# The dispatch of a mixture of experts in two parts: three samples' full blocks first, the last sample's between the blocks

## The chip, the cores and the metric

The kernel runs on one core of a Trainium2 chip. The metric is the device time of one execution in microseconds (us). PE (TensorE) multiplies and transposes, DVE (VectorE) and ACT (ScalarE) evacuate PSUM and do the elementwise work, POOL (GpSimd) does some elementwise work and issues the indirect gathers and scatters, and SP (SyncE) issues the plain DMAs. Each engine runs its own instructions in order, and semaphores join them.

## The reference, cut to what matters

The input x is 4 samples of 1024 positions with 256 channels. Three layers follow one another:

```python
x = x + softmax(theta(x) @ phi(x).T) @ g(x) @ W_out + b_out      # in each sample, width 32
t = t + nystrom_attention(layernorm(t))                         # 8 heads, 128 landmarks, 6 steps of an inverse
# mixture of experts: T = 4096 tokens, E = 16 experts, K = 2
xf = layernorm(t)
probs = softmax(xf @ W_gate); top_g, top_i = top_k(probs, 2)
for e in range(16):
    y += gates[:, e] * (gelu(xf @ W1[e]) @ W2[e])               # 256 -> 512 -> 256
t = t + y
```

Each sample's attention needs that sample alone. The inputs are seeded, so it can be counted which experts the 8192 picks go to. Picks of experts 0 to 15 in all four samples: 269 371 331 470 957 915 584 865 786 425 263 770 232 441 313 200. Of these in the first three samples: 221 285 242 373 703 665 451 696 577 333 203 515 171 332 230 147. A block is 128 picks of one expert, so there are 73 blocks that hold picks (3 3 3 4 8 8 5 7 7 4 3 7 2 4 3 2 by expert), and the kernel always runs 79.

## The kernel before, in words

For each sample `i` three stages of 8 tiles follow one another. Stage one (`s` from 0 to 9, lines L1234 to L1375) is the first attention: PE multiplies scores (L637), DVE takes the maxima (L1234), ACT the exponentials (L1074), PE turns them (`transposes`, L545), ACT copies them (L1087), PE multiplies with the values (L719) and DVE finishes the row and its norm (`rows0`, `norm0`). Stage two is the Nystrom attention's landmarks: the same pattern per head, and between its steps in each slot `s` up to four pieces of the iterative inverse (`inverse_piece`, L871 on PE, L1489 and L1490 on DVE). In each slot DVE also does a step of the routing of the sample before (`top_two`, `index`, `picks`, `one_hots`, `either`, `counted`). A slot of PE waits at `values` for `pr_used`, that is for DVE's L1499 of the head before. Stage three applies the landmarks to the 8 tiles: eight small exponentials per tile on ACT (L1079), `inverses` on DVE, `turn_inverses` on PE (L698), which spreads 8 reciprocals over 256 rows by sixteen small matmul instructions, `out_t`, `rows1` (L1386), statistics, a deviation on POOL (L400, L401), and `norm1` (L1357).

After the last sample comes the dispatch. The last rows are turned, gated (L608, L617) and routed. The picks of all 32 tiles are ranked (L961 to L967), DVE works out where each expert's blocks begin and where each pick goes (L1597 to L1617), and for 8 steps of four tiles DVE, ACT and PE build one-hot rows and multiply them into a table that says which pick stands in which row of which block (`select`, L1629 to L1634, and `place`, L977). Out of that come `token_of`, `row_of` and `expert_of`. PE runs transposes that nothing uses while it waits (lines before L985).

Then 79 blocks run, sorted by expert. For block `n` POOL gathers 128 rows (L434), PE turns them, DVE copies them (L1678), PE multiplies with W1 (L1008, `hidden`), ACT applies Gelu (L1174) and stages the next W1 (L1165), PE multiplies with W2 (L1017, `rows_out`), DVE scales by the gate (L1695), and POOL adds the rows to the output in memory by a scatter (L448). The gather of block n+4 stands ahead of the scatter of block n in POOL's queue. Blocks of one expert never hold the same token, so their scatters may be under way together. The first of another expert must wait until all scatters of the experts before it have landed; the first 8 blocks wait for the one before each. From block 8 on SP watches the landings (L537) and lets POOL go on by `scatter_ok`. All experts' weights (16 of 1 MB) are loaded by SP, more than half of them after the last sample, into memory that the attention has used.

## Time and profile before

| | us |
|---|---|
| median of 3 runs (range) | 990.86 (990.32 to 993.77) |
| the profiled execution | 986.97 |
| its span, first to last instruction | 985.2 |
| PE busy | 902.3 (92%) |
| DVE busy | 559.1 (57%) |
| ACT busy | 448.1 (45%) |
| POOL busy | 298.1 (30%) |

The busy time of an engine is summed over the span. The stages have different limits, so the time is read stage by stage: windows give the busy time in a stretch, and the timeline gives each instruction with the idle time of its engine before it and what ended that.

### The profile page before, as it was taken

What the parts mean: (1) busy time and instruction counts of PE and PEld (TensorE: products, weight loads), DVE (VectorE), ACT (ScalarE), POOL (GpSimd) and SP (SyncE); (2) the same over time, 40 slices, a digit from 0 to 9 for tenths busy, and PEclk for the clock granted to TensorE, in tenths of its full rate; (3) what the DMA queues carried; (4) which work ended last, traced back from release to release, by engine and by line L of the source; (5) the groups of instructions that cost most, each with busy time, mean ns of one, the idle gap of its engine ahead of it and who ended that gap; (6) DMA issues with size and microseconds to landing.
All of it is one profiled execution on the core that took longest, in us unless ns stands there. A gap on an engine that the chain in (4) does not pass through costs nothing.

```text
span 985.2 us, 21923 instructions
## 1 busy us (share of the span) xinstructions
PE 902.3 (92%) x7118; PEld 700.4 (71%) x7119; DVE 559.1 (57%) x1581; ACT 448.1 (45%) x1004; POOL 298.1 (30%) x343
## 2 busy tenths in 40 slices
PE   5999989899999899999899999638999999999997
PEld 3566767565767565777656676428889999999996
DVE  3577857677857588766678775694222222222222
ACT  2524367534358443348452347334434444444442
POOL 3150001060001041001131000103576676666665
PEclk9699999999999899999899999857999999999999
DMA  3100000300000200000206004581344434434341
GB/s 107 44 2 1 1 1 24 107 1 1 1 2 16 85 31 2 1 2 2 72 15 214 1 1 151 152 256 36 52 65 71 69 63 72 67 62 67 61 64 19
DMA packets 47848, 50.78 MB, mean 52 GB/s; under 512 B 11072, under 2 KB 41152, under 8 KB 47776
## 3 DMA queue, kind: packets, MB, share of 16 engines
q0 software_dynamic: 15168, 18.85, 12.1%
q1 hardware_dynamic: 32608, 30.99, 10.0%
q8 instruction: 43, 0.70, 0.3%
q14 instruction: 29, 0.24, 0.1%
HBM read 33.00 MB, written 18.78 MB: 53 GB/s over the span
## 4 chain that ended last, share of the span: by engine, by line
PE 79%; DVE 13%; issue 4%; ACT 3%; DMA 1%; POOL 1%; POOLq 0%; DVEq 0%; ACTq 0%
PE PS L1008 14%; PE PS L1017 14%; PE PS L545 12%; PE PS L871 7%; PE PS L574 6%; PE PS L637 4%; PE PS L738 3%; PE PS L648 3%; PE PS L642 3%; DVE neg_max L1234 3%; PE PS L719 3%; PE PS L724 2%; ACT arena L1079 1%; PE PS L733 1%; DVE arena L1222 1%
## 5 line engine op out<-in xcount | busy, mean ns | idle before, releaser
L400 POOL TENSOR_SCALAR aggr<-aggr 128x1 f32<-128x1 f32 x64 | 14.2, 222 | 517.8 <-DVE aggr L1354 517.8
L1234 DVE TENSOR_REDUCE neg_max<-PS 128x1 f32<-128x1024 f32 (+1 forms) x96 | 117.5, 1224 | 79.5 <-PE PS L648 27.4
L545 PE MATMUL PS<-ident,arena 128*128 128x128 f32 x1008 | 142.0, 289 | 19.4 <-DMA arena<-in_x_dram 6.5
L1008 PEld LDWEIGHTS PS<-low 128*128 128x128 f32 x1264 | 153.3, 192 | 4.6 <-DVE low L1678 0.6
L545 PEld LDWEIGHTS PS<-ident,arena 128*128 128x128 f32 x1008 | 123.7, 151 | 45.9 <-issue 36.9
L1008 PE MATMUL PS<-low 128*128 128x128 f32 x1264 | 153.8, 275 | 0.4 <-DVE low L1678 0.4
L1017 PE MATMUL PS<-arena,low 128*128 x632 | 150.0, 380 | 3.0 <-ACT low L1174 1.8
L448 POOL DMA_INDIRECT out_dram<-low,row_of x79 | 125.4, 1587 | 81.1 <-DVE low L1695 30.3
L1087 ACT COPY arena<-PS 128x1024 f32<-128x1024 f32 x96 | 98.4, 1025 | 86.9 <-PE PS L545 86.9
L1017 PEld LDWEIGHTS PS<-arena,low 128*128 128x128 f32 x632 | 114.0, 190 | 16.7 <-issue 4.4
L1174 ACT ACTIVATE low<-PS 128x512 f32<-128x512 f32 x79 | 47.2, 597 | 157.8 <-PE PS L1008 157.7
L1074 ACT ACTIVATE arena<-PS,neg_max 128x1024 f32<-128x1024 f32 x64 | 71.3, 1114 | 96.2 <-DVE neg_max L1234 96.2
L434 POOL DMA_INDIRECT low<-rows_scratch,token_of x79 | 78.1, 988 | 64.2 <-DVE token_of L1651 38.8
L1079 ACT ACTIVATE arena<-PS,neg_max 128x128 f32<-128x128 f32 x256 | 90.4, 399 | 7.6 <-DVE neg_max L1234 7.6
L1695 DVE TENSOR_SCALAR low<-PS,slot_gate 128x256 f32<-128x256 f32 x79 | 38.2, 483 | 97.3 <-issue 64.9
L1165 ACT COPY low<-arena 128x1024 f32 x79 | 82.4, 1045 | 18.2 <-issue 14.4
L1676 DVE TENSOR_TENSOR gate_parts<-low,pick_of 128x2 f32<-128x2 f32 x79 | 12.7, 161 | 125.1 <-PE PS L545 125.1
L871 PE MATMUL PS<-arena 128*128 128x256 f32 x320 | 74.4, 386 | 0.0
L871 PEld LDWEIGHTS PS<-arena 128*128 128x128 f32 x320 | 59.1, 190 | 11.2 <-issue 4.0
L574 PE MATMUL PS<-arena,low 128*128 128x512 f32 x128 | 61.7, 606 | 4.5 <-DVE arena L1492 2.6
L1051 ACT ACTIVATE arena<-PS 128x512 f32<-128x512 f32 x40 | 23.7, 595 | 83.4 <-PE PS L574 40.2
L1079 ACT ACTIVATION_READ_ACCUMULATOR arena<-PS,neg_max 128x1 f32 x256 | 60.9, 238 | 0.0
(216 smaller groups left out, 1310.3 us busy)
## 6 DMA issues: line engine op xcount, KB each, us to landing
arena<-in_L_ffn_W_dram SPq DMA_DIRECT2D x32, 512.0 KB, 8.4
arena<-in_x_dram SPq DMA_DIRECT2D x4, 1024.0 KB, 6.3
out_dram<-t SPq DMA_DIRECT2D x4, 1024.0 KB, 7.3
rows_scratch<-arena SPq DMA_DIRECT2D x4, 512.0 KB, 4.1
rows_scratch<-arena SPq DMA_DIRECT2D x8, 256.0 KB, 2.7
low<-rows_scratch,token_of POOLq DMA_INDIRECT x79, 2.8
out_dram<-low,row_of POOLq DMA_INDIRECT x79, 3.8
arena<-in_L_attn_w_qkv_dram SPq DMA_DIRECT2D x1, 768.0 KB, 4.8
```

Source lines behind the costliest of these rows:

```text
L434: pool.indirect_dma_start(xg[:, n % 4, :], None, rows_dram, bass.IndirectOffsetOnAxis(ap=token_of[:, n:n + 1], axis=0)).then_inc(xg_loaded ...
L448: pool.indirect_dma_start(out_rows, bass.IndirectOffsetOnAxis(ap=row_of[:, n:n + 1], axis=0), y_sb[:, n % 4, :], None, bounds_check=T - 1, ...
L545: mm = pe.transpose(PS[0:s.shape[1], dst_bank, n * P:n * P + s.shape[0]], s, ident[0:s.shape[0], 0:s.shape[0]])
L574: mm = pe.matmul(PS[0:m, bank, :], w[c], src[:, c, half * 512:half * 512 + 512], start=c == 0, stop=c == KC - 1)
L871: mm = pe.matmul(bank[:, o:o + 2 * M], RX[:, g, h, 0, :], RX[:, g, h].rearrange("p r m -> p (r m)"), start=True, stop=True)
L1008: mm = pe.matmul(PS[:, 2 + p, hc * P:(hc + 1) * P], w1_now[:, p, c * H + hc * P:c * H + (hc + 1) * P], xgT[:, p, c, :], start=c == 0, stop ...
L1017: mm = pe.matmul(PS[:, 6 + p, 0:D], hT[:, p, c, :], w2_sb[:, bass.ds(e * (HC * D) + c * D, D)], start=c == 0, stop=c == HC - 1)
L1074: act.activation(Pm[:, u % 2, :], src, ACT.Exp, bias=neg_max[:, u % 2, 0:1], accum_out=row_sum[:, u % NT:u % NT + 1]).then_inc(s_exp, 1)
L1079: ins = act.activation(Pm[:, u % 2, o:o + M], src[:, o:o + M], ACT.Exp, bias=neg_max[:, u % 2, h:h + 1], accum_out=head_sum[:, u % 2, h:h ...
L1087: act.copy(PT[:, u % 2, :], PS[:, 2:4, :].rearrange("p b n -> p (b n)")).then_inc(t_act, 1)
L1165: act.copy(w1_now[:, p, :], w1_sb[:, bass.ds(e * (KC * H), KC * H)]).then_inc(w1_staged, 1)
L1234: dve.tensor_reduce(dst, src, AX.X, ALU.max, negate=True).then_inc(s_max, 1)
```

## The change

The 24 tiles of the first three samples are dispatched during the last sample. Each expert's picks among them fill `floor(count/128)` full blocks, 40 by the counts above (1 2 1 2 5 5 3 5 4 2 1 4 1 2 1 1); at least 32 (`SURE`) whatever the inputs. The picks that fill no block stand aside and join the picks of the last sample in the late blocks (33 of them hold picks: 2 1 2 2 3 3 2 2 3 2 2 3 1 2 2 1). The blocks run in this order, early ones of experts 0 to 15 and then late ones of experts 0 to 15. Ranks of the early picks are taken between stages one and two of the last sample, their one-hot rows are made by DVE and multiplied out by POOL (`early_vals`) in stage two, and PE places them there (six times eight matmuls). The tables for 32 blocks are made in stage three, and POOL gathers the first four blocks there. The routing of each sample is done in stage one of the next. The first 20 blocks are written out, and between them PE, ACT and DVE do what is left of the last sample: turning, gate, routing, ranks, one-hot rows and the second table. The weights are loaded in an order that follows the experts, nine of them before the blocks begin; most buffers move in memory for that. In stage three POOL spreads the reciprocals over 256 columns and PE turns them as two squares of 128; `rows1` and `norm1` stand earlier in a tile and its statistics are split in two. The transposes that nothing uses are gone.

```diff
+    OPEN = 5
...
+        EARLY = TT - NT
+        FULL = 2 * EARLY * P // P
+        SURE = (2 * EARLY * P - E * (P - 1)) // P
+        SURE = SURE - SURE % 4
+        EARLY_COLS, LATE_COLS = FULL + E, COLS - SURE
...
+            def early_vals(k):
+
+                b, mine = k % 2, slice(k * 2 * ST, (k + 1) * 2 * ST)
+                pool.wait_ge(hot_made, k + 1)
+                if k >= 2:
+                    pool.wait_ge(sel_used, k - 1)
+                pool.tensor_tensor(hot_val[b], hot_hi[b].unsqueeze(1).broadcast_to([P, 2, 2 * ST, EARLY_COLS]),
+                                   vals[:, :, mine].unsqueeze(3).broadcast_to([P, 2, 2 * ST, EARLY_COLS]), ALU.mult).then_inc(vals_made, 1)
...
+                def spread_inverses(t):
+
+                    pool.wait_ge(inv_ready, i * NT + t + 1)
+                    if t >= 2:
+                        pool.wait_ge(inv_mm, i * NT + t - 1)
+                    by_place = head_inv[:, t % 2, :].rearrange("p (a g b) -> p g a b", g=NG, b=2)
+                    for g in range(NG):
+                        pool.tensor_copy(inv_spread[:, t % 2, g * P:(g + 1) * P].rearrange("p (a b d) -> p a b d", a=2, b=2),
+                                         by_place[:, g].unsqueeze(3).broadcast_to([P, 2, 2, HD])).then_inc(inv_spread_ready, 1)
+
...
+                    if i == B - 1 and t == NT - 4:
+
+                        pool.wait_ge(tokens_ready, 1)
+                        pool.wait_ge(gates_stored, 16)
+                        pool.wait_ge(xn2_stored, 16 * 3 * (B - 1))
+                        pool.wait_ge(q_mm, B * 4)
+                    if i == B - 1 and NT - 4 <= t < NT:
+                        gather(t - (NT - 4))
...
+                    if n + 4 == SURE:
+
+                        pool.wait_ge(tokens_ready, 2)
+                        pool.wait_ge(gates_stored, 16 * 2)
+                        pool.wait_ge(xn2_stored, 16 * 3 * B)
+                        pool.wait_ge(out_stored, 16 * B)
...
+            i = B - 1
+
+            sp.wait_ge(s_mm, i * UNITS + 3)
+            sp.wait_ge(tpg_mm, 2 * B)
+            sp.wait_ge(xb_ready, B)
+            store_out(i - 1)
+            both_in(0, 1)
+
+            sp.wait_ge(s_mm, i * UNITS + NT)
+            sp.wait_ge(pr_used, i * UNITS + NT)
+            sp.wait_ge(g_ready, B)
+            both_in(2, 3)
+
+            sp.wait_ge(gates_made, 1)
+            sp.dma_start(gate_cols[:, 0:EARLY], gates[:, 0:EARLY]).then_inc(gates_stored, 16)
+
+            sp.wait_ge(pv_mm, i * UNITS + 2 * NT)
+            both_in(4, 5)
+
+            sp.wait_ge(y_head_mm, B)
+            sp.wait_ge(sel_used, EARLY // ST)
+            both_in(6, 7, 8)
+            store_rows(i, 0, 4)
+            loaded(range(9))
+
+            sp.wait_ge(s_mm, B * UNITS)
+            both_in(9)
+            first_in(10)
...
+            sp.wait_ge(gates_made, 2)
+            sp.dma_start(gate_cols[:, EARLY:TT], gates[:, EARLY:TT]).then_inc(gates_stored, 16)
 
             sp.wait_ge(release_ready, 1)
-            with sp.Fori(IN_TURN, BLOCKS) as n:
-                landed = [sp.value_load(release[0:1, bass.ds(n, 1), u:u + 1].rearrange("p o u -> p (o u)"), min_val=16,
-                                        max_val=16 * (ROUNDS + 1)) for u in range(4)]
-                for u in range(4):
...
-                    for g in range(NG):
-                        for j in range(QUADS):
-                            h = g * GH + j
-                            mm = pe.matmul(PS[HD * j:HD * j + HD, 0, g * P:(g + 1) * P], head_inv[:, t % 2, PLACE[h]:PLACE[h] + 1].broadcast_to([P, HD]),
-                                           ident[:], start=True, stop=True, tile_position=(0, HD * j))
-                    mm.then_inc(inv_mm, 1)
...
+                def early_place(k):
+
+                    pe.wait_ge(vals_made, k + 1)
+                    pe.wait_ge(pr_used, i * UNITS + NT + k + 2)
+                    if k == 0:
+                        pe.wait_ge(starts_made, 1)
+                        pe.transpose(PS[0:1, 0, 288:288 + BW], block_expert[0:BW, :], ident[0:BW, 0:BW])
+                    for j in range(2 * ST):
+                        mm = pe.matmul(PS[:, 0, 512 - 2 * EARLY_COLS:512], hot_lo[k % 2][:, j, :], hot_val[k % 2][:, :, j, :],
+                                       start=j == 0, stop=j == 2 * ST - 1)
+                    mm.then_inc(sel_used, 1)
...
+            aside = {0: lambda: turn_high(B - 1), 2: lambda: gate(B - 1), 4: lambda: gate_turned(B - 1), 9: late_ranks,
+                     12: late_turns, 17: late_place}
...
+            pe.wait_ge(pr_used, B * UNITS)
             turn_rows(1, 0, 1)
             hidden(0, 0, False)
-            for u in range(4):
-                expert_block(0, u, False)
-            with pe.Fori(1, ROUNDS) as i:
+            for r in range(OPEN):
+                for u in range(4):
+                    expert_block(r, u, r >= 1)
+                    if 4 * r + u in aside:
+                        aside[4 * r + u]()
+            pe.wait_ge(tables_ready, 2)
...
+            def late_exps():
+
+                act.wait_ge(probs_in, 2)
+                act.activation(probs_b, probs_b, ACT.Exp)
+                act.activation(gates[:, EARLY:TT], gates[:, EARLY:TT], ACT.Exp).then_inc(probs_exp, 1)
+
+            aside = {0: lambda: bulk(23, xT[:, 1, 512:1024], j=B - 1), 8: late_exps}
...
+                def early_starts():
+
+                    dve.wait_ge(rank_mm, 1)
+                    for j in range(B - 1):
+                        dve.tensor_copy(run_a[:, j * NT:(j + 1) * NT], PS[:, 1, j * E * NT:(j + 1) * E * NT].rearrange("p (e t) -> p t e", t=NT))
+                    alone(dve.tensor_copy(col_e[:, 0, :], PS[:, 1, EARLY * E:EARLY * E + E]))
+                    dve.memset(small[:, 43:44], 0.0).then_inc(rank_read, 1)
+                    alone(dve.tensor_copy(col_ei[:], col_e[:, 0, :]))
...
+                def early_added(k):
+
+                    dve.wait_ge(sel_used, k + 1)
+                    src = PS[:, 0, 512 - 2 * EARLY_COLS:512].rearrange("p (a n) -> p a n", a=2)
+                    if k == 0:
+                        dve.tensor_copy(expert_row[0:1, 0, :], PS[0:1, 0, 288:288 + BW])
+                        dve.tensor_copy(early_parts[:], src).then_inc(sel_added, 1)
+                    else:
+                        dve.wait_ge(sel_added, k)
+                        dve.tensor_tensor(early_parts[:], src, early_parts[:], ALU.add).then_inc(sel_added, 1)
+
+                def early_hot(k):
+
+                    b, mine = k % 2, slice(k * 2 * ST, (k + 1) * 2 * ST)
+                    over_row = lambda ap, n: ap.unsqueeze(1).broadcast_to([P, 2 * ST, n])
+                    over_col = lambda ap, n: ap.unsqueeze(2).broadcast_to([P, 2 * ST, n])
+                    if k >= 2:
+                        dve.wait_ge(vals_made, k - 1)
+                        dve.wait_ge(sel_used, k - 1)
+                    dve.tensor_tensor(hot_lo[b], over_row(iota_lo[:], P), over_col(pos_lo[:, mine], P), ALU.is_equal)
+                    dve.tensor_tensor(hot_hi[b], over_row(iota_hi[:, 0:EARLY_COLS], EARLY_COLS), over_col(pos_hi[:, mine], EARLY_COLS),
+                                      ALU.is_equal).then_inc(hot_made, 1)
+
+                def route(s):
+
+                    if s == 3:
...
+                def route(s):
+
+                    if s == 3:
+                        for t in range(NT):
+                            top_two(i, t)
+                    elif s in (4, 5):
+                        for t in range(4 * (s - 4), 4 * (s - 4) + 4):
+                            index(i, t)
+                    elif s == 6:
+                        picks(i)
+                        keep(i)
+                    elif s == 7:
+                        one_hots(i)
+                    elif s == NT:
+                        either(i)
+                    elif s == NT + 1:
+                        counted(i)
+
...
+                def early_steps(s):
+
+                    if s == 0:
+                        early_run()
+                    elif s == 1:
+                        alone(positions(run_a, weighed_a, early, slice(0, 2 * EARLY)))
+                    elif s == 2:
+                        early_hot(0)
+                    if 2 <= s < EARLY // ST + 1:
+                        early_hot(s - 1)
+                    if s == 3:
+                        dve.wait_ge(kept, B - 1)
+                        gates_in(probs_a, early, slice(0, EARLY))
+                    elif s == 7:
+                        dve.wait_ge(probs_exp, 1)
+                        gates_out(probs_a, slice(0, EARLY))
+
...
+            aside = {0: lambda: bulk(22, xT[:, 0, 512:1024], j=B - 1), 1: lambda: releases(0, IN_TURN, release_early[:, IN_TURN:SURE]),
+                     3: lambda: gate_out(B - 1), 5: late_top, 6: late_index, 7: late_picks, 8: late_counts, 9: late_gates,
+                     10: late_starts, 11: late_run, 13: late_rest, 14: lambda: late_hots(0), 15: lambda: late_hots(1),
+                     18: late_tables, 19: lambda: releases(1, SURE, release_late[:])}
```

## Rows read from the trace of the kernel before

**Rows 1.** Windows: us; busy PE, PEld, DVE, ACT, POOL; clock, DMA, GB/s

```profile
603.43:619.50 16.07, 16.07 (x209) 12.49 (x210) 11.78 (x29) 15.49 (x71) 2.37 (x6) 1.00 0.33 107
...
553.39:578.70 25.31, 25.31 (x188) 19.16 (x184) 20.82 (x69) 8.87 (x12) 0.00 (x0) 1.00 0.00 1
...
351.00:357.00 6.00, 6.00 (x75) 3.93 (x73) 5.59 (x13) 3.95 (x7) 2.96 (x6) 1.00 0.01 3
...
740.00:960.00 220.00, 220.00 (x1533) 207.74 (x1533) 61.65 (x236) 96.87 (x118) 151.88 (x118) 1.00 0.42 66
...
320.00:340.00 20.00, 16.71 (x91) 10.35 (x88) 12.00 (x23) 7.75 (x13) 2.37 (x6) 0.83 0.12 42
```

**Rows 2.** Timeline of PE: start, us, engine, line, operation, tiles, count, idle before

```profile
340.65 1.05 PE L608 MATMUL PS<-arena,wgate_sb 128*32 128x256 f32 x16
...
605.95 0.62 PE L698 MATMUL PS<-ident,head_inv 128*32 128x128 f32 x16
...
607.47 1.04 PE L545 MATMUL PS<-ident,arena 128*128 128x128 f32 x8
...
629.41 1.03 PE L738 MATMUL PS<-low 128*128 128x256 f32 x4
...
654.35 1.22 PE L977 MATMUL PS<-low 128*128 128x160 bf16 x8 [8.42 <-ACT low L1142]
...
678.27 3.84 PE L1008 MATMUL PS<-low 128*128 128x128 f32 x32 [0.37 <-DVE low L1678]
```

**Rows 3.** Timeline, DVE, end of the last sample

```profile
630.48 0.42 DVE L1386 TENSOR_TENSOR t<-PS,arena 128x256 f32<-128x256 f32 x1
...
632.91 0.41 DVE L1357 TENSOR_SCALAR arena<-t,aggr 128x256 f32<-128x256 f32 x1 [0.80 <-POOL aggr L401]
```

**Rows 4.** Timeline, PE and then DVE, in stage two of the last sample

```profile
559.14 0.64 PE L719 MATMUL PS<-arena 128*32 128x128 f32 x16
...
558.58 0.25 DVE L1499 TENSOR_SCALAR low<-PS,row_inv 128x32 f32<-128x32 f32 x1
```

**Rows 5.** Timeline, DVE, operations of the dispatch

```profile
638.98 0.62 DVE L1280 MAX8 top_now<-logits_now 128x8 f32<-128x16 f32 x7
...
651.77 0.82 DVE L1629 TENSOR_TENSOR low<-iota_hi,pos_hi 128x640 bf16<-128x640 bf16 x1
...
652.52 1.22 DVE L1631 TENSOR_TENSOR low<-iota_lo,pos_lo 128x1024 bf16<-128x1024 bf16 x1
```

**Rows 6.** Timeline, POOL and then DVE, when both work in stage one

```profile
367.37 0.72 POOL L423 TENSOR_TENSOR arena<-arena,low 128x256 f32<-128x256 f32 x1
...
369.01 4.53 POOL L406 TENSOR_TENSOR arena<-arena,low 128x2048 f32<-128x2048 f32 x1
...
367.44 0.81 DVE L1357 TENSOR_SCALAR arena<-arena,aggr 128x256 f32<-128x256 f32 x1 [0.80 <-POOL aggr L401]
```

**Rows 7.** Timeline, POOL, scatters of the block stage

```profile
685.53 1.65 POOL L448 DMA_INDIRECT out_dram<-low,row_of  x1 [5.93 <-DVE low L1695]
...
703.73 1.59 POOL L448 DMA_INDIRECT out_dram<-low,row_of  x1 [1.78 <-DVE low L1695]
...
709.19 1.59 POOL L448 DMA_INDIRECT out_dram<-low,row_of  x1 [2.58 <-DMA out_dram<-low,row_of]
...
718.55 1.59 POOL L448 DMA_INDIRECT out_dram<-low,row_of  x1 [1.85 <-DVE low L1695]
...
765.74 1.59 POOL L448 DMA_INDIRECT out_dram<-low,row_of  x1 [0.96 <-DVE low L1695]
...
770.34 1.59 POOL L448 DMA_INDIRECT out_dram<-low,row_of  x1 [1.72 <-DVE gate_parts L1676]
...
773.52 1.59 POOL L448 DMA_INDIRECT out_dram<-low,row_of  x1 [0.30 <-issue]
```

**Rows 8.** Timeline, ACT, the change of its table

```profile
668.75 1.28 ACT L1156 ACT_TABLE_LOAD   x1
```

**Rows 9.** Timeline, SP, the store of the gates

```profile
650.70 1.38 SPq L529 DMA_DIRECT2D rows_scratch<-gates  x1
```

702 lines of the change are left out of this document (418 added, 284 removed).

## The prediction

> **What bounds the kernel now.** I read the windows first, stage by stage. In the block stage PE is busy for the whole of 740 to 960 us [rows 1]: 1533 matmul instructions at 26 per block (16 hidden, 2 turned, 8 out) are 59.0 blocks in 220.0 us, 3.73 us each, and 79 blocks at that rate are 294.7 us. Four slots of stage two of the last sample take 25.31 us, 6.33 each, with PE full and DVE busy for 20.82; in stage one DVE has 5.59 of 6.00 beside a full PE; four tiles of stage three take 16.07, 4.02 each, with PE full and ACT busy for 15.49 [rows 1]. So each stage is bound by PE, with DVE or ACT right behind it. The one place where nothing is near full is the dispatch. The PE timeline shows it: the last output projection starts at 629.41 and the first hidden layer at 678.27 [rows 2]. Those 48.9 us are what the change is after.
>
> **What goes.** After it the first hidden layer needs only the end of the attention. From the DVE timeline: row 7 of the last sample is added at 630.48, its norm starts at 632.91 (it waits for POOL) and ends near 633.3 [rows 3]. DVE then has a small product and one copy of 256 columns (0.42, as any such operation in [rows 3]) to do, and the split statistics move all by 0.1 to 0.3. That puts the hidden layer at 634.1 to 634.2, if tables, rows and weights are there, where it was 678.27: **-44.1**. The transposes that nothing uses lie inside this gap. The first weights are issued in stages one to three, and the first four gathers some 15 us early, so I cost them at nothing; the cover is that time.
>
> **What the block stage takes over.**
> - PE's moved work: sixteen gate matmuls at 1.05 [rows 2], eight transposes about 1.0 [rows 2], the smaller turns and ranks 1.0, and seventeen placements of 96 columns. Eight of 160 columns took 1.22 [rows 2] at half clock, so 1.4. Together 4.4, of which I count 3, since PE also stalls for scatters among the first ten blocks.
> - DVE's moved work: it has about 2.4 us free per block before the next block's copy is late (61.65 busy in 220 [rows 1] is 1.05 of 3.73, and the copy must be done when the hidden layer begins). `late_starts`, some twenty small chained operations, is about 4.3, so 1.9 late; `late_tables` 0.6 late. Total 2.5, from 0 to 6.
> - ACT needs exponentials again between two Gelus: two table loads at 1.28 [rows 8] plus 0.6, against some 1.8 free in a block: 1.5.
> - SP lets scatter 8 go only after it has sent the late gates, which DVE makes behind block 9. The store took SP 1.38 for 4096 rows [rows 9]. POOL's scatters and the gathers behind them wait: 2, from 0 to 7.
> - The clock: between 320 and 340 us a pause of 1.8 us was followed by a mean of 0.83 [rows 1], which is 6.8 us at half rate, 3.4 lost. The pause before the first block is over 3 us, so 3.5, from 0 to 4.
> - About 7 MB of weights and stores are still on their way when the first gathers and scatters start: 1, from 0 to 6.
> - **More changes of expert.** Order decides how often a scatter must wait for all landings before it. Before, the 79 blocks have 15 such changes, after it 31 (15 in the 40 early blocks, one between, 15 in the late). Scatter 21 is the first of expert 5: it starts 4.60 after scatter 20; the next, not a first, 3.18 later [rows 7], and 3.18 is POOL's own minimum. Against 3.73 a first loses 0.87 and another wins back 0.55. Blocks 28 to 72 have 23 firsts and 22 others: 23 x 0.87 - 22 x 0.55 = 7.9. How much backlog is free? In the first eight, each waiting for the one before, scatter 4 starts 18.20 after scatter 0 [rows 7], where four blocks are 14.9: 3.3 behind, and there PE first stalls, for a gather that stood behind the scatters. So 7.9 - 3.3 = 4.6.
>
> Sum: 3 + 2.5 + 1.5 + 2 + 3.5 + 1 + 4.6 = **+18.1**.
>
> The Trainium skill ("ScalarE: Activation LUTs", rules for kernel authors) budgets 2.7 us for every switch of set. The load here took 1.28 [rows 8]; with the page's figure this term would be 4.3 instead of 1.5.
>
> **What the last sample takes over.** In stage two PE and DVE hand over closely: W of a head is ready at 558.83 (L1499) and PE uses it at 559.14 [rows 4], so DVE has 0.3 us to spare, beyond the 0.6 of routing that now goes. `early_hot` is a comparison of 1024 and one of 512: 1.13 and 0.6 by the rows of 1024 and 640 less overlap [rows 5], 1.7 per step and two steps in slot 2. The excess over 0.9 falls on PE: 2.6 in slot 2, 1.7 in slot 3 (the gates are there too), 0.85 in each of slots 4 to 6, 0.2 in slot 7, together 7.1. The six placements on PE are 0.6 each, 3.5. `positions` in slot 1 (768 elements twice and six small ones, 2.75) costs 1.8, `early_run` in slot 0 0.9. Ranks and `early_starts` before stage two: DVE has gaps there, 0.8. The added sums at the end of stage two 0.9, `early_tables` with its dozen small operations on DVE in stage three 1. Sum **+16**, between 7 (DVE catches up in its waits) and 26 (POOL's multiplications are late: 2048 elements took 4.53 [rows 6], so 1024 about 2.4, and twice that would exceed its slot).
>
> **Routing in stage one** of samples 1 to 3. It brings eight maxima (seven took 0.62 [rows 5]), the indices and four products, near 4 us of DVE per sample, to the stage where DVE has 0.41 of 6.00 free [rows 1]. The stage ends in a wait for POOL of 0.8 [rows 6] and in smaller waits for PE, which hide the last steps, and PE runs up to 1.6 us ahead of DVE. I take 1.3 per sample, **+4**, from 0 to 9. In stage two, from which it goes, PE is the bound: nothing is won outside the last sample.
>
> **Stage three.** Sixteen instructions (0.62 busy [rows 2]) become two transposes: 1.04 for eight [rows 2], so 0.26. PE wins 0.2 to 0.3 a tile while PE is the bound, which is some four to five tiles of eight, and ACT stops it at about 3.8 of 4.02 us (15.49 in four tiles is 3.87 with overlaps, and no gap but a wait for DVE per tile [rows 1]): -1.0 per sample. POOL's two copies (0.45 each from 0.72 for 256 [rows 6]) come after the reciprocal and 2 us ahead of their use, also behind a deviation or a gather. The earlier `rows1` shortens the chain of the last three tiles by 0.5 per sample. **-6** in all, from -10 to +4.
>
> **Sum.** -44.1 + 18.1 + 16 + 4 - 6 = -12.0. The span of 985.2 becomes 973.2, the profiled execution 986.97 becomes 975.0. The median lies 3.9 above that execution; the same saving from it gives 990.86 - 12.0 = 978.9, say 979.
>
> **Rivals.**
> - *Most of the moved work is hidden* (chance 0.25). DVE's excess in stage two is taken up by its waits (7 for 16), the routing by the slack of stage one (0), the block stage takes 11: -44.1 + 11 + 7 + 0 - 6 = -32, 959 us. For it: DVE is busy for 20.82 of 25.31 in stage two [rows 1]. Against: the margin of 0.3 there.
> - *The scatters become the bound* (0.12, the slower side). If a first starts 5.5 us after the one before (as scatter 5, at 709.19, did after scatter 4, at 703.73; the first eight average 33.02 / 7 = 4.72 [rows 7]), 23 x 1.77 - 22 x 0.55 - 3.3 = 25.3 instead of 4.6, and the early blocks add some 4: 979 + 25 = 1004. It cancels the gain at 0.87 + 12 / 23 = 1.4 over 3.73, that is 5.1 between scatters; from 5.3 on the kernel is slower by 0.5%. Against: 4.60 once the backlog is gone.
> - *POOL holds stage two* (0.13). POOL's products and DVE's comparisons run at once. A norm that took 0.41 [rows 3] took 0.81 while POOL was multiplying [rows 6]. If the two lengthen each other so, the early hot rows take 4.8 on POOL and 3 on DVE, and six slots gain 1.6 each: +10, 989. The Trainium skill ("GPSIMD Engine Reference", key points) says that POOL shares its SBUF interfaces with VectorE, with contention when a DVE instruction has two SBUF inputs or runs in a 2-port mode; both comparisons have two such inputs. One row agrees so far.
> - *The change doesn't do what it says* (0.05): the first tables, weights or gathers are not there at 634 plus what the last sample has grown, and PE waits a further 10 to 20 us behind SP's queue: 989 to 999.
> - My forecast has 0.45.
>
> **How the numbers follow.** Forecast 979, its own range 970 to 988 from the bounds of its terms. For 8 in 10 I reach down to 962, short of the first rival's end, and up to 995. A measurement of this kernel can tell about 0.5%, 5 us, from no change. Faster than 985.9: nearly all of the first rival and 0.40 of my 0.45, and some of the third: 0.72. Within: 0.16. Slower than 995.8: the scatters and part of the last rival, 0.12.
>
> **What would show it.** In the profile of the changed kernel: the first L1008 of the blocks some 4 us after the last projection, with the clock at 0.5 for up to 7 us; slots of stage two in the last sample at 7.5 to 8 us instead of 6.33, with PE waiting for W; scatters near 4.6 apart in blocks 28 to 72 and PE waiting for gathers there; stage-three tiles at 3.8 instead of 4.0. The forecast is wrong if stage two keeps 6.9 us slots, if scatter spacing leaves 4.1 to 4.8, or if PE waits before the first block.

## The result, and the profile of the changed kernel

| | before | changed |
|---|---|---|
| median of 20 runs each, us | 990.25 | 994.50 |
| range | 985.65 to 997.06 | 990.83 to 997.88 |
| span of the profiled execution | 985.2 | 993.4 |

The ratio of the two is 1.0037, with a 95% interval of 1.0022 to 1.0053: a little slower, clear of no change, though by less than the 0.5% that I had named as the least a measurement can tell. I had forecast 979, 1.2% faster. Each ratio below is to the kernel before, run beside it on the same chip. The changed kernel itself did not run beside the variants, so "less than the changed kernel" is always the difference between a variant's ratio and 1.0037.

Some words that come back below: a maximum is DVE's first operation on a tile's or a head's scores, and a stage is measured from its first maximum to that of the next stage; a slot is the stretch from one maximum to the next, counted from 0; a first is a scatter that must wait until all before it have landed; the landing is the end of a scatter's transfer.

The gap in front of the blocks is gone as predicted. The timeline of PE in the changed kernel (columns: start, duration, engine, line, operation, tiles, count, idle time before and what ended it) answers [rows 2]. Its first six rows belong to the steps of stage two of the last sample:

```profile
start us, us, engine line op out<-in xcount [idle before <-releaser]
548.27 2.08 PE L1028 MATMUL PS<-arena 128*128 128x128 f32 x8 [2.15 <-DVE small L1773]
...
559.57 0.65 PE L852 MATMUL PS<-arena 128*32 128x128 f32 x16 [2.40 <-DVE low L1823]
...
570.29 0.29 PE L894 MATMUL PS<-ident,block_expert 80*1 80x80 f32 x1 [4.32 <-issue]
570.37 1.06 PE L896 MATMUL PS<-arena 128*128 128x128 bf16 x8
...
580.98 0.61 PE L896 MATMUL PS<-arena 128*128 128x128 bf16 x8 [1.51 <-DVE low L1823]
...
611.87 0.61 PE L896 MATMUL PS<-arena 128*128 128x128 bf16 x8 [2.19 <-DVE low L1823]
...
646.84 0.44 PE L680 MATMUL PS<-ident,inv_spread 128*128 128x128 f32 x2 [1.19 <-POOL inv_spread L491]
...
653.65 1.10 PE L871 MATMUL PS<-low 128*128 128x256 f32 x4
...
658.84 3.53 PE L1140 MATMUL PS<-low 128*128 128x128 f32 x21 [2.76 <-DVE low L1995]
```

The last projection starts at 653.65 and the first hidden layer at 658.84, 5.2 us later instead of 48.9. But 658.84 is only 19.4 us before the old 678.27, not 44: the samples have become longer. And from scatter 0 to scatter 78 the blocks take 320.5 us instead of 294.5.

**Where the samples grew.** Read by the starts of DVE's maxima. Stage two of the last sample took 51.5 us and takes 72.8. Stage one of samples 1 to 3 took 48.65, 49.86 and 50.02, and takes 52.06, 52.26 and 50.91 (+6.7 in these two traces; other traces of the same code sum to 150.7 instead of 148.5, and to 156.8 instead of 155.2). Stage three of samples 0 to 2 took 51.87, 52.22 and 51.87, and takes 49.22, 49.23 and 49.23 (-8.3); that of the last sample, from first to last maximum, 33.06 and now 36.42 (+3.4). Everything also starts 2.2 us later (first maximum at 19.73, before 17.56). The windows of slots 1, 2, 3 and 5 of stage two and of the whole stage answer the second window of [rows 1] (6.33 a slot, PE full):

```profile
core 0: us, PE busy (x) PEld busy (x) DVE busy (x) ACT busy (x) POOL busy (x), PEclk, DMA share, GB/s
546.39:559.34 12.95, 8.90 (x34) 5.84 (x34) 6.88 (x23) 2.81 (x4) 0.00 (x0) 0.74 0.00 0
559.34:570.10 10.76, 6.40 (x46) 4.82 (x46) 9.84 (x17) 2.22 (x3) 3.01 (x2) 0.91 0.01 2
570.10:580.75 10.65, 9.18 (x55) 6.86 (x55) 7.41 (x19) 2.22 (x3) 2.48 (x2) 0.77 0.00 0
590.25:598.12 7.87, 6.93 (x54) 5.26 (x54) 6.71 (x17) 2.22 (x3) 1.90 (x2) 1.00 0.01 3
533.18:605.98 72.80, 58.81 (x403) 42.12 (x403) 56.68 (x125) 20.99 (x31) 10.95 (x6) 0.88 0.00 1
```

The granted clock (the figure behind POOL's) was 1.00 there before. Now it is 0.74, 0.91 and 0.77 in three slots, and 0.82 in slot 4. Narrower windows show where it fell to the lower of its two levels, 1.2 instead of 2.4 GHz: inside PE's idle of 2.15 us, inside that of 4.32, and 0.8 us after the end of that of 1.51. It didn't fall after the idle of 2.40: PE's work in slot 2 ran at 2.4 GHz, and the 0.91 there comes from the idle of 4.32 at the slot's end. The eight placements show the two levels: 1.06 us at 570.37, and 0.61 at 580.98 and in the later slots. PE's work behind the idles of 2.15, 2.40 and 1.51:

```profile
548.27:554.00 5.73, 5.73 (x15) 3.66 (x16) 1.13 (x4) 0.79 (x3) 0.00 (x0) 0.50 0.00 0
559.57:565.97 6.40, 6.39 (x46) 4.79 (x46) 5.51 (x12) 2.22 (x3) 0.00 (x0) 1.00 0.01 3
580.98:585.00 4.02, 4.02 (x30) 3.03 (x31) 2.05 (x5) 1.75 (x4) 1.25 (x1) 0.60 0.00 0
```

**Where the blocks grew.** POOL's timeline, the scatters alone (L528), answers [rows 7]:

```profile
667.74 1.65 POOL L528 DMA_INDIRECT out_dram<-low,row_of  x1 [7.40 <-DVE low L2009]
...
675.05 1.59 POOL L528 DMA_INDIRECT out_dram<-low,row_of  x1 [4.36 <-DMA out_dram<-low,row_of]
...
682.90 1.58 POOL L528 DMA_INDIRECT out_dram<-low,row_of  x1 [4.97 <-DMA out_dram<-low,row_of]
...
707.84 1.59 POOL L528 DMA_INDIRECT out_dram<-low,row_of  x1 [1.79 <-DMA out_dram<-low,row_of]
...
716.44 1.59 POOL L528 DMA_INDIRECT out_dram<-low,row_of  x1 [5.71 <-SPq L664]
```

These are scatters 0, 1, 2, 7 and 8. The first intervals are 7.31 and 7.85, where four took 18.20 before. Two windows of the changed kernel, from the first hidden layer to scatter 0 and from scatter 0 to scatter 2 (the last three figures are clock, DMA share and GB/s):

```profile
658.84:667.74 8.90, 8.90 (x57) 8.64 (x58) 2.73 (x10) 3.39 (x5) 1.09 (x2) 0.81 1.07 364
667.74:682.90 15.16, 13.83 (x107) 12.09 (x105) 4.76 (x22) 7.51 (x11) 5.23 (x4) 1.00 0.94 283
```

The first stretch took 7.26 before, at a clock of 1.00: here the half clock costs some 1.6 ahead of scatter 0. In the second the weights are still loading.

Scatter 8 starts 8.60 after scatter 7 and is released by SP's L664 (the count of landings), which SP reached only after it had stored the late gates at 712.03. In the whole, scatters 0 to 8 take 48.7 us (before 36.2) and blocks 28 to 72 take 179.1 (before 168.4). The chain of work that ended last, by engine, in the kernel before and then in the changed one:

```profile
PE 79%; DVE 13%; issue 4%; ACT 3%; DMA 1%; POOL 1%; POOLq 0%; DVEq 0%; ACTq 0%
PE 65%; DVE 16%; issue 7%; DMA 6%; ACT 2%; POOL 2%; SPq 0%; POOLq 0%; DVEq 0%; ACTq 0%
```

What PE lost there went to transfers, to stretches in which nothing that the profile shows was waited for ("issue"), and to DVE.

### The profile page after: what moved, and what is told of

It is laid out like the page before. It is cut to its first block, busy times and chain, and to the rows that moved or that the text cites. A ratio compares the mean times of both kernels' runs of the same rounds, so it can differ in the third digit from the quotient of the medians.

```text
span 993.4 us, 20907 instructions
## 1 busy us (share of the span) xinstructions
PE 904.6 (91%) x6644; PEld 694.3 (70%) x6645; DVE 561.7 (57%) x1610; ACT 437.4 (44%) x975; POOL 332.4 (33%) x413
## 4 chain that ended last, share of the span: by engine, by line
PE 65%; DVE 16%; issue 7%; DMA 6%; ACT 2%; POOL 2%; SPq 0%; POOLq 0%; DVEq 0%; ACTq 0%
PE PS L1149 11%; PE PS L1140 11%; PE PS L680 11%; PE PS L1033 8%; PE PS L712 6%; DMA out_dram<-low,row_of 4%; DVE neg_max L1402 3%; PE PS L786 3%; PE PS L775 3%; PE PS L780 2%; PE PS L871 2%; PE PS L852 2%; DMA low<-rows_scratch,token_of 2%; PE PS L857 1%; ACT arena L1246 1%
## 5 line engine op out<-in xcount | busy, mean ns | idle before, releaser
L528 POOL DMA_INDIRECT out_dram<-low,row_of x79 | 126.7, 1604 | 107.0 <-SPq L664 35.6
L1149 PE MATMUL PS<-arena,low 128*128 x632 | 155.9, 391 | 6.7 <-issue 4.6
L1140 PE MATMUL PS<-low 128*128 128x128 f32 x1264 | 156.4, 278 | 2.9 <-DVE low L1995 2.8
L1149 PEld LDWEIGHTS PS<-arena,low 128*128 128x128 f32 x632 | 116.5, 194 | 24.8 <-issue 11.3
L491 POOL COPY inv_spread<-head_inv 128x128 f32<-128x128 f32 x64 | 18.1, 312 | 262.2 <-DVE head_inv L1499 262.1
L1033 PE MATMUL PS<-arena 128*128 128x256 f32 x320 | 77.1, 395 | 0.0
L712 PE MATMUL PS<-arena,low 128*128 128x512 f32 x128 | 65.4, 637 | 5.0 <-DVE arena L1786 2.4
L1033 PEld LDWEIGHTS PS<-arena 128*128 128x128 f32 x320 | 61.1, 196 | 12.3 <-issue 4.3
```

Source lines behind the costliest of these rows:

```text
L528: pool.indirect_dma_start(out_rows, bass.IndirectOffsetOnAxis(ap=row_of[:, n:n + 1], axis=0), y_sb[:, n % 4, :], None, bounds_check=T - 1, ...
L712: mm = pe.matmul(PS[0:m, bank, :], w[c], src[:, c, half * 512:half * 512 + 512], start=c == 0, stop=c == KC - 1)
L1033: mm = pe.matmul(bank[:, o:o + 2 * M], RX[:, g, h, 0, :], RX[:, g, h].rearrange("p r m -> p (r m)"), start=True, stop=True)
L1140: mm = pe.matmul(PS[:, 2 + p, hc * P:(hc + 1) * P], w1_now[:, p, c * H + hc * P:c * H + (hc + 1) * P], xgT[:, p, c, :], start=c == 0, stop ...
L1149: mm = pe.matmul(PS[:, 6 + p, 0:D], hT[:, p, c, :], w2_sb[:, bass.ds(e * (HC * D) + c * D, D)], start=c == 0, stop=c == HC - 1)
```

## The experiments

A caution for single traces: the changed kernel and seven of the kernels below have the same code up to stage two of the last sample. From the first maximum to there they took 513.4 to 513.9 us in five profiled executions (the changed kernel's among them) and 516.6 to 516.7 in the other three, and the first maximum itself lay between 17.4 and 20.0. So 3 us of such a sum, and the 2.2 at the start, say nothing of a change. A single stage can differ by 1.6 to 1.7 in the same way. The stages named below are compared one by one.

**1. The new stage three alone, in the kernel before.** First the squares with DVE's old order (POOL's copies, and on PE this):

```diff
-                    for g in range(NG):
-                        for j in range(QUADS):
-                            h = g * GH + j
-                            mm = pe.matmul(PS[HD * j:HD * j + HD, 0, g * P:(g + 1) * P], head_inv[:, t % 2, PLACE[h]:PLACE[h] + 1].broadcast_to([P, HD]),
-                                           ident[:], start=True, stop=True, tile_position=(0, HD * j))
-                    mm.then_inc(inv_mm, 1)
+                    transposes(pe, 0, [inv_spread[:, t % 2, g * P:(g + 1) * P] for g in range(NG)]).then_inc(inv_mm, 1)
```

> The kernel before with one part of the change alone: POOL spreads the reciprocals over 256 columns and PE turns them as two squares; DVE's order stays. My prediction gave this 0.2 to 0.3 us a tile where PE is the bound. Theory one (PE is the bound in stage three and the squares alone make the samples' stage three shorter, which was 2.7 us per sample for samples 0 to 2 in the changed kernel): about -2 us per sample, 982 to 984. Rival (the gain of 2.7 came from rows1 and norm1 standing earlier, and the squares only add a wait for POOL): 990, within 1.5 of the kernel before.

Measured: 986.62 against 990.0, ratio 0.9970 (0.9944 to 0.9997). Stage three of samples 0 to 2 took 50.38, 50.74 and 50.38, some 1.5 less each. Then with the new order of DVE as well:

```diff
                     if 1 <= s < NT:
                         inverses(s)
+                    if s >= 3:
+                        rows1(s - 3)
+                    if s >= 4:
+                        norm1(s - 4)
...
-                    if s >= 3:
-                        rows1(s - 3)
-                    if s >= 4:
-                        norm1(s - 4)
+                    if s >= 3:
+                        stats1(s - 3)
                     if s + 2 < NT:
                         maxima(2 * NT + s + 2)
+                    if s >= 3:
+                        moments1(s - 3)
```

> The kernel before with the squares and also the earlier rows1 and norm1 and the split statistics of the changed kernel. Stage three of samples 0 to 2 was 2.6 to 3.0 us shorter in the changed kernel. Theory one (that part is independent of the dispatch and holds for the last sample too): 4 x 2.7 = -10.8, 979.5. Rival (the last sample's stage three grew by 3.4 us in the changed kernel because of this part, not because of the tables and gathers in it): -8 + 3 = -5, 985.

Measured: 982.4, ratio 0.9919 (0.9890 to 0.9948). The stages took 49.54, 49.55 and 49.54, and the last sample's 32.25. In the last sample the maxima in DVE's timeline stand 3.75 apart, where four tiles took 16.07 before:

```profile
606.28 1.23 DVE L1246 TENSOR_REDUCE neg_max<-PS 128x8 f32<-128x1024 f32 x1 [1.00 <-PE PS L665]
...
610.03 1.23 DVE L1246 TENSOR_REDUCE neg_max<-PS 128x8 f32<-128x1024 f32 x1 [0.58 <-PE PS L665]
```

So this half of the change is sound by itself and makes the kernel before 0.8% faster. That the last sample's stage three grew by 3.4 in the changed kernel is not its doing.

**2. The routing of samples 0 and 1 back in stage two.**

```diff
-                    if i >= 1:
+                    if i == B - 1:
                         route(s)
...
                     if i == B - 1:
                         early_steps(s)
+                    elif i >= 1:
+                        route(s + 2)
```

> The changed kernel with the routing of samples 0 and 1 put back into stage two of samples 1 and 2; that of sample 2 stays in stage one of the last sample, where the dispatch needs it. Stage one of samples 1 and 2 was 3.4 and 2.4 us longer in the changed kernel. Theory one (the routing is the cause, and stage two hides it as before): -5.8, 988.7. Rival (the buffers' new places or the offset at the start are the cause): no change, 994.5.

Measured: 993.23, ratio 1.0034 (1.0005 to 1.0063), no difference from the changed kernel that could be told. The three stage ones went from 155.2 to 151.4 together, but stage two of samples 1 and 2 took 51.79 and 53.43 instead of 51.55 each. The expected -5.8 was wrong. Of the 3.8 that the stage ones gave back, stage two took 2.1, but 1.9 of that is in sample 2's alone, and stage two of sample 0, which never has routing in it, took 53.2 instead of 51.55 in runs 7, 9 and 10. So what the place of the routing costs isn't shown by this run. What shows it better is stage one of sample 1 at the same granted clock: 48.65 (0.96, the kernel before) and 50.46 (0.97, run 10), 50.25 (0.93, run 5) and 52.06 (0.93, the changed kernel), +1.8 both times.

**3. The one-hot values on ACT instead of POOL.** Six small activations a step (two scaled by row, four by tile) in place of POOL's product:

```diff
-                    for k in range(EARLY // ST):
-                        early_vals(k)
...
                     turned(NT + s)
+                    if i == B - 1 and s >= 3:
+                        early_vals(s - 3)
```

> The changed kernel with the six products of stage two (the one-hot values) on ACT, as six small activations a step, instead of one POOL multiplication of 1024 elements. POOL is then idle while DVE makes the one-hot rows. Rival of the prediction (POOL and DVE hold each other up through shared access: the comparison of 512 took 2.38 us instead of 0.68 beside POOL's product): stage two of the last sample, 72.8 us, loses 6 to 10. Other theory (the sum of DVE's work and the late handover to PE is the cause, whoever multiplies): ACT's six activations, about 1.5 us a step, sit between its copy and its exponentials, and stage two stays at 71 to 76.

Measured: 997.2, ratio 1.0086 (1.0053 to 1.0120); stage two 74.86. In the changed kernel's DVE timeline one comparison of 512 was held up beside POOL's product, the other was not:

```profile
565.70 0.68 DVE L1651 TENSOR_TENSOR arena<-iota_hi,pos_hi 128x512 bf16<-128x512 bf16 x1
566.30 1.22 DVE L1650 TENSOR_TENSOR arena<-iota_lo,pos_lo 128x1024 bf16<-128x1024 bf16 x1
567.44 2.38 DVE L1651 TENSOR_TENSOR arena<-iota_hi,pos_hi 128x512 bf16<-128x512 bf16 x1
```

With POOL idle both take 0.69:

```profile
566.23 0.69 DVE L1665 TENSOR_TENSOR arena<-iota_hi,pos_hi 128x512 bf16<-128x512 bf16 x1
...
567.97 0.69 DVE L1665 TENSOR_TENSOR arena<-iota_hi,pos_hi 128x512 bf16<-128x512 bf16 x1
```

So the two engines do hold each other up, and it costs 1.7 us once, in slot 2: that slot took 10.70 here, and 12.40 in run 4, where POOL multiplied and the slot before was the same as here (11.3 us, clock 0.85). (In the changed kernel's own trace it took 10.76, with PE's work at the full clock.) The other slots weren't lengthened so. On ACT the work is dearer: slots 5 and 6 are 10.16 instead of 7.87, with PE idle for 1.65 instead of 0.93 before each placement and a clock of 0.83 instead of 1.00. Here POOL is the better place for it. The Trainium skill says ("GPSIMD Engine Reference", key points) that POOL shares its SBUF interfaces with VectorE, with contention for instructions such as this comparison; the trace agrees, with 2.38 against 0.69, for one instruction of twelve. The comparison of 1024 at 566.30, which had begun 0.17 before POOL's product (at 566.47, for 2.81), took its usual 1.22.

**4. What the order of the scatters costs.** In both kernels every pick's row is scattered to a row of its own, and all waits for landings go. Both kernels leave out that the rows are added to the output:

```diff
-                pool.indirect_dma_start(out_rows, bass
+                pool.indirect_dma_start(own_rows, bass
...
-                if n >= IN_TURN:
-                    pool.wait_ge(scatter_ok, n - IN_TURN + 1)
-                elif n >= 1:
-                    pool.wait_ge(y_stored[(n - 1) % 4], ((n - 1) // 4 + 1) * 16)
```

> The changed kernel with each pick's row scattered to a row of its own in another memory, so that no scatter has to wait for another one (the waits for landings are gone; what is left out: the rows are not added to the output). It prices all that the order of the scatters costs the changed kernel. Theory one (the waits at each change of expert hold the blocks up; from scatter 0 to scatter 78 they take 320.5 us, against 294.5 before, and the rest of the last sample's work between the blocks costs some 9): -15 to -17, 978. Rival (the pieces of the last sample, the half clock and the weights' loads cost the 26 us): -3 to -5, 990.

> The kernel before with the same edit: rows scattered to rows of their own, no waits for landings. PE is at its bound from the twelfth block on, so only the stalls of the first ten blocks can go (scatter 0 to 8 took 38 us, where eight blocks are 29.8): -4, from -2 to -8, 986.

Measured: the changed kernel so 969.47, ratio 0.9787 (0.9750 to 0.9824); the kernel before so 983.55, ratio 0.9931 (0.9902 to 0.9959). Against the changed kernel's 1.0037 the order costs it 25 thousandths, 24.7 us; the kernel before, 6.8. The scatters show the same: from 0 to 78 they take 293.6 in the changed kernel without the order and 288.9 in the kernel before, so **all of the last sample's work between the blocks, ACT's tables behind scatter 0 and the loads cost 4.7 us where no scatter waits**, and the order adds 26.9 to the one and 5.6 to the other. The half clock ahead of scatter 0 (1.6) isn't in that stretch. POOL's timeline in the changed kernel without the order (scatters 0, 1 and 2), where the same weights are loading, with the window from scatter 0 to scatter 2:

```profile
666.79 1.65 POOL L524 DMA_INDIRECT own_rows<-low,row_of  x1 [6.12 <-DVE low L2003]
...
671.38 1.59 POOL L524 DMA_INDIRECT own_rows<-low,row_of  x1 [1.63 <-DVE low L2003]
...
675.11 1.58 POOL L524 DMA_INDIRECT own_rows<-low,row_of  x1 [0.84 <-DVE low L2003]
...
666.79:675.11 8.32, 8.32 (x68) 7.04 (x67) 3.46 (x17) 4.76 (x7) 5.24 (x5) 1.00 1.04 331
```

Beside the same loads these start 4.59 and 3.73 apart, instead of 7.31 and 7.85.

**5. More firsts in the kernel before.** 14 more blocks are marked as firsts of an expert, so 27 scatters from block 8 on wait for all before them, 23 of them in blocks 28 to 72, as in the changed kernel:

```diff
+            for n in (16, 31, 36, 38, 39, 43, 45, 50, 53, 57, 60, 66, 70, 72):
+                dve.memset(more_firsts[0:1, n:n + 1], 1.0)
...
+                link(dve.tensor_tensor(first_of[0:1, 0, :], first_of[0:1, 0, :], more_firsts[0:1, :], ALU.max))
```

> The kernel before with 14 more blocks marked as firsts of an expert, so that from block 8 on 27 scatters wait for all landings before them instead of 13, as in the changed kernel, and 23 of them in blocks 28 to 72 as there. It prices the order of the experts alone. My prediction's term: 7.9 less the backlog that is free, +4.6, 994.5. Rival (each first costs more than I took, since the chain of landing, release and start is 4.7 to 5.2 us instead of 4.60): +12 to +16, 1004.

Measured: 1000.96, ratio 1.0110 (1.0074 to 1.0146), +10.9. By the traces blocks 28 to 72 take 179.1 us, as in the changed kernel (that they agree to the tenth is luck: in the other kernels with the new order it is 176.9 to 178.6); 168.4 in the kernel before, and 168.0 and 168.1 in the two without the order. Scatters 42 to 45 of this run (43 and 45 are firsts):

```profile
853.34 1.59 POOL L449 DMA_INDIRECT out_dram<-low,row_of  x1 [0.30 <-issue]
...
858.03 1.59 POOL L449 DMA_INDIRECT out_dram<-low,row_of  x1 [1.82 <-SPq L538]
...
861.21 1.59 POOL L449 DMA_INDIRECT out_dram<-low,row_of  x1 [0.30 <-issue]
...
865.94 1.59 POOL L449 DMA_INDIRECT out_dram<-low,row_of  x1 [1.85 <-SPq L538]
```

**6. The landings ahead of the late gates' store.**

```diff
-            sp.wait_ge(gates_made, 2)
-            sp.dma_start(gate_cols[:, EARLY:TT], gates[:, EARLY:TT]).then_inc(gates_stored, 16)
-
             sp.wait_ge(release_ready, 1)
-            landings(release_early[:, IN_TURN:SURE], SURE - IN_TURN)
+            landings(release_early[:, IN_TURN:IN_TURN + 8], 8)
+            sp.wait_ge(gates_made, 2)
+            sp.dma_start(gate_cols[:, EARLY:TT], gates[:, EARLY:TT]).then_inc(gates_stored, 16)
+            landings(release_early[:, IN_TURN + 8:SURE], SURE - IN_TURN - 8)
```

> The changed kernel with one move on SP: the landings of scatters 8 to 15 are watched before the late gates are stored, so scatter 8 no longer waits for them (it started 8.60 after scatter 7). Theory one (that wait costs what it shows, 4, less what PE's backlog gives back): -3, 991.5. Rival (PE's stall there is made up by the ones behind it, since the scatters are in line at every first): within 1, 994.

Measured: 988.09, ratio 0.9984 (0.9964 to 1.0004), 5.2 us less than the changed kernel. Scatter 8 starts 3.19 after scatter 7 instead of 8.60, and scatters 0 to 8 take 42.0 instead of 48.7. A move of three lines was worth more than the wait that I had priced at 2.

**7. The weights of experts 13 to 15 after the first twelve scatters.** On top of that move:

```diff
-            first_in(13)
-            first_in(14)
...
-            landings(release_early[:, IN_TURN:IN_TURN + 8], 8)
+            landings(release_early[:, IN_TURN:IN_TURN + 4], 4)
+            both_in(13, 14, 15)
```

> The changed kernel with the landings of scatters 8 to 11 watched before the late gates are stored, as in the run that moved them, and the weights of experts 13 to 15 (3 MB) loaded only after these landings. In that run the first eight scatters took 42.0 us, with 7.35, 6.79 and 5.92 between some, while DMA was at its full share. Theory one (the loads of the weights lengthen the landings of scatters that wait for one another): the first eight take 37 to 39, 3 to 5 us less than with the landings moved alone, 984. Rival (the first scatters wait for rows from PE at half clock and for gathers): no change against that run, 988.

Measured: 986.74, ratio 0.9980 (0.9956 to 1.0004). The first eight intervals fall to 36.4 us, what the kernel before needs (36.2):

```profile
674.31 1.59 POOL L528 DMA_INDIRECT out_dram<-low,row_of  x1 [2.14 <-DMA out_dram<-low,row_of]
...
678.94 1.58 POOL L528 DMA_INDIRECT out_dram<-low,row_of  x1 [1.74 <-DMA out_dram<-low,row_of]
```

So the loads did lengthen the landings, and only because the first scatters wait for one another did that matter. But scatter 12 now starts 7.91 after scatter 11, behind SP's loads, and of the 5.6 us won 1.6 are left at scatter 78 (310.4 against 312.0). In the times no gain over run 6 can be told: the theory was right about the cause and wrong about the total.

**8. PE kept busy in stage two of the last sample.** Transposes that nothing uses ahead of its waits:

```diff
+                    if s >= 2:
+                        fill({2: 16, 3: 28, NT: 14}.get(s, 6), mine[0] if s < NT else pieces[-1])
                     if i == B - 1 and s >= 3:
                         early_place(s - 3)
...
+                    if s == 1:
+                        fill(12, mine[0])
```

> The changed kernel with transposes that nothing uses on PE ahead of its waits in stage two of the last sample (12 and 16 in slots 1 and 2, 28 in slot 3, six in slots 4 to 7, 14 in slot 8), sized to the idle times that its trace shows there, 0.13 us each. Nothing else changes. Theory one (each idle of PE lowered the granted clock, 0.74 to 0.91 in those slots, and some 10 of the 21.3 us that stage two grew by are PE's half rate and not DVE's work): stage two 72.8 becomes 63 to 66, total -8, 986. Rival (DVE's added work holds the slots and the half rate lies in PE's slack): stage two stays within 2 us.

Measured: 984.76, ratio 0.9953 (0.9930 to 0.9975), 8.3 us less than the changed kernel. Windows of its slots 1 to 3:

```profile
544.58:554.49 9.91, 8.76 (x60) 6.55 (x58) 6.86 (x23) 2.81 (x4) 0.00 (x0) 1.00 0.00 0
554.49:565.26 10.77, 9.61 (x74) 7.86 (x74) 9.85 (x18) 2.22 (x3) 3.01 (x2) 1.00 0.01 2
565.26:573.73 8.47, 7.81 (x61) 5.96 (x61) 7.41 (x19) 2.22 (x3) 2.48 (x2) 1.00 0.00 0
```

The clock is 1.00 throughout, and the slots are 9.91, 10.77 and 8.47 instead of 12.95, 10.76 and 10.65; slot 4 is 7.87 instead of 9.50. The middle one is the same in both because PE's work in it ran at the full clock in the changed kernel's trace too; DVE is busy for 9.85 of its 10.77 us. In run 4's trace, where PE worked at 1.2 GHz behind the same idle of 2.4 us, that slot took 12.40 (and slot 1 11.31 instead of 12.95, so that the whole stage was 72.9 against 72.8):

```profile
558.00:570.40 12.40, 8.03 (x46) 5.93 (x46) 9.94 (x18) 2.22 (x3) 3.01 (x2) 0.79 0.00 1
```

Stage two takes 65.95 instead of 72.80, and the stretch between the second and the third maximum of stage three 12.22 instead of 13.43.

**9. More work for DVE there.** The comparison of 1024 is made twice in each of the six steps:

```diff
+                    dve.tensor_tensor(again[:], over_row(iota_lo[:], P), over_col(pos_lo[:, mine], P), ALU.is_equal)
                     dve.tensor_tensor(hot_lo[b], over_row(iota_lo[:], P), over_col(pos_lo[:, mine], P), ALU.is_equal)
```

> The changed kernel with the comparison of 1024 elements (1.22 us) made twice in each of the six early steps, once into a buffer that nothing reads: 7.3 us more of DVE work in stage two of the last sample. Theory one (the handover between DVE and PE leaves no slack, so every us of DVE work in a slot lengthens it): stage two +7.3, and more where PE's clock falls further, 1002 to 1005. Rival (DVE catches up in its waits for PE, 1.1 of 7.86 us in slots 6 and 7): +2 to +4, 998.

Measured: 1003.54, ratio 1.0141 (1.0099 to 1.0182). Stage two takes 83.00, +10.2 for 7.3 us of DVE work. There is no slack, and the clock adds to it: slot 2, with two such comparisons, is 2.39 longer for 2.36 more of DVE, and slots 5 and 6 are 2.6 and 2.5 longer for 1.13 each, with clocks of 0.83 and 0.84 instead of 1.00.

**10. Both mends.** Run 6 and run 8 together.

> The changed kernel with two mends together: the landings of scatters 8 to 15 ahead of the late gates, and the filling transposes in stage two of the last sample. If each is worth what the single runs show or are expected to show (-5 and -8) and they add up: 980, level with the kernel before with the new stage three (982). If the clock is the same pool for both (a fall avoided in stage two comes later): 985 to 988.

Measured: 978.67, ratio 0.9899 (0.9869 to 0.9929). The two add up (-0.53% and -0.84% make 0.9900), and this version is faster than the kernel before by 1.0%. Windows of its stage two and of the steady blocks:

```profile
534.15:600.10 65.95, 61.45 (x483) 46.21 (x483) 56.68 (x124) 21.01 (x31) 10.96 (x6) 1.00 0.00 1
...
740.00:960.00 220.00, 215.92 (x1482) 201.05 (x1481) 63.11 (x249) 93.39 (x115) 145.87 (x114) 1.00 0.39 62
```

In 740 to 960 us PE has 1482 matmuls, 57.0 blocks, where [rows 1] has 1533, 59.0 blocks. Blocks 28 to 72 take 176.9 us, 8.5 more than in the kernel before: most of the order of the scatters is still paid. The intervals of this one and of the kernel before with the new stage three (0.9890 to 0.9948) overlap, so which of the two is faster isn't shown.

## Why the prediction was wrong, point by point

The forecast was -12.0 and the medians say +4.2; the profiled spans say +8.2, since the two executions don't lie alike to their medians. The signs of all terms were right, and the sizes of two of them were not. Of the 20.2 us between the forecast and the spans, the block stage has 9.5 and stage two of the last sample 5.3. Three steps failed there: PE's half clock was left out of stage two, the wait behind SP's store was taken for 2, and the scatters between two firsts were taken to win back 0.55 each.

- **What goes (-44.1): right.** 5.2 us from the last projection to the first hidden layer, 4.7 predicted.
- **The last sample's stage two (+16): 21.3, a missing term.** What DVE's added work costs was about right: with the clock kept up the stage is 14.4 longer (65.95 against 51.5), and DVE's busy time in it grew by 15.2 (41.47 to 56.68). I had let DVE catch up by 0.9 a slot, of which 0.6 is the routing that left; run 9 shows that hardly more is caught up. What I left out was PE's clock: run 8 gives 6.9 us in the stage and 1.2 behind it. I counted half rate only for the pause before the blocks, though [rows 1] had shown me 0.83 after a pause of 1.8 us, and though I forecast that PE would wait in every slot.
- **Routing in stage one (+4, up to 9):** the three stages grew by 6.7 in these two traces, and run 2 couldn't tell a net cost. At the same clock sample 1's grew by 1.8, where I took 1.3. The range held, as far as single traces can say.
- **Stage three (-6): right where it stands alone.** 0.9919 is -8.0 us in the kernel before. In the changed kernel three samples gave 8.3, and the last one took back 3.4. All of that lies in its first two intervals between maxima, 2.52 and 13.43 us where they took 1.64 and 10.87. There the last two placements, their sums on DVE and the early gates still run, PE stands 2.19 us before the last placement (611.87 above) and then goes on at half clock, which run 8 prices at 1.2. The other 2.2 are these steps by their place in the trace; no run prices them alone. The tables on DVE come later, where the other five intervals together take 20.5 as before, 0.7 more than in run 1. The gathers on POOL come from 641 us on: PE stood 1.19 us once for reciprocals that POOL spread late (646.84), which I had costed at nothing.
- **The block stage (+18.1): 26.0 from scatter 0 to scatter 78 and 1.6 ahead of it, and the shares were the wrong way round.** PE's, DVE's and ACT's work, the half clock and contention, 11.5 together, cost 4.7 where no scatter waits (run 4), and the clock 1.6 ahead of that (3.5 predicted). (The 1.4 for seventeen placements doesn't follow from its row, which gives 1.6 at its half clock; nothing hangs on it.) What was to be small was large:
  - *SP's late store (2):* 6.7 us in the scatters, 5.2 in the time (run 6). I took it for a wait that the backlog takes up.
  - *Contention (1, up to 6):* 5.6 in the first eight intervals (run 7). I had looked for it in gathers, and it sat in the landings: each of the first eight scatters waits for the one before, so the time of a landing adds up. That reason stood in my own text, for another step.
  - *More changes of expert (4.6):* 10.7 in blocks 28 to 72 (run 5 reproduces it with nothing else changed). A first cost what I took, 4.57 after the one before (4.60 predicted). The failed step is that every other scatter "wins back 0.55", by POOL's minimum of 3.18: they came 3.37 apart. 14 of the 22 did come at 3.18 to 3.20, and the other eight at 3.35 to 4.57, because a scatter can be earlier than PE's pace only as far as it is late. 23 x 0.84 - 22 x 0.36 = 11.4, and the free backlog of 3.3 wasn't there to take off.
- **The start (+2.2 in the trace)** isn't the change's: executions of the same code differ by as much.
- **The rivals.** *Most of it is hidden* fell in run 9. *The scatters become the bound* had the right mechanism and the wrong price: not 5.5 for a first, but hardly a gain in between. Its own term, blocks 28 to 72, was to be 25.3 and is 10.7. The whole order costs 21.3 more than before, but SP's store and the loads are in that sum, so that it comes near 25.3 is luck. I gave the rival 0.12, mainly because one first stood at 4.60, and didn't vary what the others win back. *POOL and DVE hold each other up* is real and worth 1.7 us, not 10. ACT's tables: two loads of 1.28 around the late exponentials, as expected; a third, for the first Gelu, stands at 661.41 between the first hidden layer and scatter 0, where the kernel before had it in its gap [rows 8].

## What to carry to other kernels

Price the order of serialised transfers by their chain, not by their mean: a scatter that must wait loses its whole excess, and the ones behind it win back only what they are late, so the number of waiting ones counts nearly in full. When work is moved into a stage where two engines take turns, its cost is nearly its own duration (14.4 us for 15.2 here). Add what PE's half clock costs behind the pauses that the work causes, 8.1 us here, and try filling the pauses with transposes first, since that was worth 0.8%. Look at what a sequencer (SP) does between two loops of releases: one wait for a late result in front of them held all that stood behind, and three moved lines were worth 0.5%.

## What the runs showed of the hardware that I had not expected

- PE's clock fell in or soon after idles of 1.51, 2.15, 2.19 and 4.32 us in the last sample of the changed kernel; it didn't after one of 2.40 there, nor after those of 0.93 in slots 5 and 6, nor after one of 1.46 at 588.86 in the kernel before. The same idle can go either way: in run 4's trace PE worked at 1.2 GHz at once behind the one of 2.39 (sixteen matmuls in 1.07 us instead of 0.65). In the kernel before, behind an idle of 1.79 at the start of stage one, eight transposes took 1.06 us in sample 1 and 1.94 in sample 2, as the clock fell 1.4 us after the idle's end in the one and inside the idle in the other. Stages of the same code differ with it: sample 1's stage one took 48.65 us at a clock of 0.96 there, and 50.25 at 0.93 in run 5. Transposes without a use kept the clock at 1.00 through idles of up to 1.12 that remained.
- A scatter of 128 rows that waits for the landing of the one before mostly started 4.6 to 4.8 us after it; with a DMA share of 0.94 (283 GB/s) beside it, 7.31 and 7.85. Scatters that don't wait started 4.59 and 3.73 apart beside the same loads (1.04, 331 GB/s).
- The comparison of 512 bf16 elements on DVE took 2.38 instead of 0.69 beside a product on POOL, in one of the steps alone.
